# Where sixteen joins and eight statistics stand among the products of a mixture-of-experts layer

## The reference

```python
x = layernorm(x + attention(x))              # an online-gradient attention, 32 steps in sequence
gu = einsum('th,ehf->etf', x, w_gate_up)     # 8 experts, 2 of them for each token
routed = combine(silu(g) * u @ w_down)       # weights of the top two
shared = silu_and_mul(x @ w_sh_gate_up) @ w_sh_down      # one expert for all tokens, width 1024
x = layernorm(x + routed + shared)           # the last thing computed
```

## Time and profile before

| what | us |
|---|---|
| median of three runs | 683.67 |
| lowest and highest of them | 683.64, 685.2 |
| the profiled execution, whole | 685.18 |
| its span | 683.4 |
| TensorE busy in the span | 661.5 (97%) |
| VectorE busy | 450.9 (66%) |
| ScalarE busy | 316.7 (46%) |
| GpSimd busy | 308.0 (45%) |

### The profile page before, as it was taken

How to read it: one execution, slowest core, us unless ns; L and a number is a source line. 1 busy time by engine, 2 the same in 40 slices (tenths; PEclk the granted TensorE clock), 3 DMA queues, 4 the chain that set the end, 5 groups by cost and what they waited for, 6 DMA issues and landing times.

```text
span 683.4 us, 16572 instructions
## 1 busy us (share of the span) xinstructions
PE 661.5 (97%) x6792; PEld 527.2 (77%) x6792; DVE 450.9 (66%) x784; ACT 316.7 (46%) x552; POOL 308.0 (45%) x314
## 2 busy tenths in 40 slices
PE   9999999999999999999999999999999999999895
PEld 7767777776777777787887888888887888788684
DVE  5875865776844465398957544644466788888864
ACT  5343434445454432531033556755676554544353
POOL 0747657767735431011005335443552245665634
PEclk9999999999999999999999999999999999999998
DMA  8212233231542541100064578677549743253323
GB/s 280 91 35 77 84 100 98 97 112 52 160 128 81 156 139 36 46 0 1 1 246 117 178 265 296 207 249 261 181 165 348 268 148 93 93 184 94 108 78 123
DMA packets 66575, 93.53 MB, mean 137 GB/s; under 512 B 17024, under 2 KB 32128, under 8 KB 66496
## 3 DMA queue, kind: packets, MB, share of 16 engines
q1 hardware_dynamic: 60816, 73.81, 32.5%
q0 software_dynamic: 5680, 18.62, 9.3%
HBM read 68.61 MB, written 23.79 MB: 135 GB/s over the span
## 4 chain that ended last, share of the span: by engine, by line
PE 66%; DVE 15%; issue 7%; POOL 7%; ACT 4%; DVEq 0%; POOLq 0%; ACTq 0%
PE bank L1365 8%; PE bank L1216 7%; PE zbank L1439 6%; PE wbank L1439 6%; PE bank L1476 6%; PE bank L1271 4%; PE zbank L1324 3%; PE zbank L1353 3%; PE wbank L1324 3%; PE wbank L1353 2%; PE zbank L1452 2%; PE bank L1324 2%; PE wbank L1250 2%; PE zbank L1234 2%; POOL za L2062 2%
## 5 line engine op out<-in xcount | busy, mean ns | idle before, releaser
L2094 POOL TENSOR_TENSOR xl<-RAW,xh 128x1024 fp32r<-128x1024 f32 x23 | 55.5, 2411 | 123.0 <-ACT xh L1896 122.9
L2111 POOL DMA_INDIRECT xg<-x1d,idxu x39 | 42.1, 1079 | 71.1 <-DVE idxu L1024 41.2
L1977 ACT ACTIVATE ah<-sg 128x512 fp32r<-128x512 f32 x36 | 22.7, 632 | 107.2 <-DVE sg L1627 107.2
L1617 DVE TENSOR_TENSOR GL<-RAW,GH 128x1024 fp32r<-128x1024 f32 x36 | 43.2, 1224 | 11.0 <-ACT GH L1891 9.6
L1216 PE MATMUL bank<-xh,GH 128*128 128x512 f32 x112 | 47.7, 426 | 0.8 <-DVE kS L1517 0.8
L2136 POOL DMA_INDIRECT xg<-yd,SI x32 | 32.6, 1018 | 34.6 <-DVE x L1751 29.0
L1216 PE MATMUL bank<-xl,GH 128*128 128x512 f32 x112 | 44.1, 394 | 0.1
L1365 PE MATMUL bank<-xh,ah 128*128 128x512 f32 x104 | 42.1, 405 | 2.0 <-DVE x L1703 1.8
L1216 PE MATMUL bank<-xh,GL 128*128 128x512 f32 x112 | 43.9, 392 | 0.0
L1629 DVE TENSOR_TENSOR al<-sg,ah 128x512 fp32r<-128x512 f32 x36 | 27.0, 749 | 25.1 <-ACT ah L1977 25.1
L1365 PE MATMUL bank<-xh,al 128*128 128x512 f32 x104 | 40.7, 391 | 0.0
(11 more groups left out here) (387 smaller groups left out, 2029.5 us busy)
## 6 DMA issues: line engine op xcount, KB each, us to landing
RAW<-in_wgu SPq DMA_DIRECT2D x13, 1024.0 KB, 6.8
yd<-RAW SPq DMA_DIRECT2D x39, 256.0 KB, 5.3
RAW<-in_wsgu SPq DMA_DIRECT2D x14, 512.0 KB, 5.7
RAW<-in_wd SPq DMA_DIRECT2D x13, 512.0 KB, 5.9
xr<-in_xT SPq DMA_DIRECT2D x16, 256.0 KB, 4.6
x<-in_xtok SPq DMA_DIRECT2D x16, 256.0 KB, 4.3
x1d<-x SPq DMA_DIRECT2D x16, 256.0 KB, 2.7
RAW<-in_wsd SPq DMA_DIRECT2D x8, 512.0 KB, 5.6
```

The source lines that it names most:

```text
L1617: e.tensor_tensor(GL[:, w % 2, k:k + 2, :], gate_raw(w, k), GH[:, w % 2, k:k + 2, :].bitcast(F32), ALU.subtract).then_inc(*mark("low", "g" ...
L2094: e.tensor_tensor(DL[:, w % 2, :, :], draw[:, raw_of(w), :, :], DH[:, w % 2, :, :].bitcast(F32), ALU.subtract).then_inc(*mark("low p", "d" ...
L2111: e.indirect_dma_start(place(s), None, x1d, bass.IndirectOffsetOnAxis(ap=idxu[:, LINES[s]:LINES[s] + 1], axis=0)).then_inc(*mark(f"dma xg{ ...
```

## The change

Only the list of steps changes; every instruction stays. In `side`, join 11 goes from behind product 1 of block 6 to behind product 3, and the joins after it move on: 12 behind product 4 of block 6, 13 and 14 behind products 3 and 4 of block 7. Join 15 leaves the blocks: it now stands behind the third of the last eight tiles' down products, between the statistics of tiles 13 and 14. Preloads 10 and 11, which need joins 14 and 15, move with them. Of the statistics, those of tile 1 leave block 2 for block 3, those of 2 go to block 4, 3 stays there, 4 and 5 stand in block 5, 6 in block 6, 7 in block 7. So block 2 has one tile's statistics where it had two, and block 5 has two where it had one; blocks 3, 4, 6 and 7 keep their number.

```diff
-    side = {(2, 1): "f0", (2, 5): "f1", (2, 3): "j3", (2, 4): "j4", (3, 1): "f2", (3, 3): "j5", (3, 4): "j6", (4, 1): "f3", (4, 5): "f4", (4, 3): "j7",
-            (4, 4): "j8", (5, 1): "f5", (5, 3): "j9", (5, 4): "j10", (6, 1): "j11", (6, 5): "f6", (6, 3): "j12", (6, 4): "j13",
-            (7, 1): "f7", (7, 5): "j14", (7, 3): "j15"}
+    side = {(2, 1): "f0", (2, 3): "j3", (2, 4): "j4", (3, 1): "f1", (3, 3): "j5", (3, 4): "j6", (4, 1): "f2", (4, 5): "f3", (4, 3): "j7",
+            (4, 4): "j8", (5, 1): "f4", (5, 5): "f5", (5, 3): "j9", (5, 4): "j10", (6, 1): "f6", (6, 3): "j11", (6, 4): "j12",
+            (7, 1): "f7", (7, 3): "j13", (7, 4): "j14"}
...
-    for n in range(4):
-        preload(8 + n, FREE[n])
+    preload(8, FREE[0])
+    preload(9, FREE[1])
...
     for n, i in enumerate(last_down(3, 3, (4, 5, 6, 7))):
+        if n == 0:
+            preload(10, FREE[2])
+        if n == 2:
+            join(15)
+            preload(11, FREE[3])
         finish(i, 4 + n)
```

## The result

| | before | changed |
|---|---|---|
| median, us (7 runs each) | 684.75 (683.64 to 685.97) | 681.99 (681.29 to 682.33) |
| ratio, 95% interval | | 0.9962 (0.9952 to 0.9972) |
| profiled execution, span | 683.4 | 680.3 |
| M: block 2's first matmul to the last tile's division | 107.73 | 104.77 |
| D: the last tile's statistics to its division | 1.90 | 3.41 |

The account below looks back on a forecast made before the run. TensorE, busy in 97% of the span, was taken as the bound, so only its waits and the end counted. -4.2 - 0.8 + 0.5 + 1.1 = -3.4 us took the median from 683.67 to 680.3 us, range 679.2 to 683.0.

Parts of the forecast that it names:

- Block 6, -4.2: Block 6: without join 11 ahead of add 5, TensorE's wait and the slow matmuls behind it go, -4.2 us.
- Block 2, -0.8: Block 2: one tile's statistics fewer, add 5 earlier, the wait for add 7 gone, no collision, -0.8 us.
- The tie that I had worked out: Block 2: GpSimd's power instruction at 577.77 against VectorE's `pairs` subtraction at 577.76; GpSimd should lose.
- The rival: Block 2: GpSimd's big subtraction first, holding VectorE's mix low; +1.1 in place of -0.8, 682.2 us; chance 0.14.
- Block 5, +0.5: Block 5: a second pair of statistics ahead of add 5 makes product 3 later, +0.5 us, 0.8 at most.
- The end, +1.1: Last tiles: late join 14 and join 15 delay the statistics and GpSimd's small instructions, +1.1 us, between 0.4 and 1.6.
- join 14's 0.4: End: join 14 starts tile 12's statistics 0.7 us late; GpSimd wins back 0.35, so at least 0.4 remains.
- join 15's 0.7: End: the share of the +1.1 us put on join 15, between the statistics of tiles 13 and 14.
- nobody is held: End: case in which join 15 and GpSimd's small instructions do not block each other; the cost stays at 0.4 us.
- held to the join's end: End: case in which GpSimd's small instructions wait for join 15; tile 14's start 1.2 to 1.7 us late, less 0.25.
- The clock in block 2: Block 2 rival: GpSimd wins, TensorE idles some 1.4 us and its clock falls; 683.9 us, chance 0.07.
- the three pairs agree: Evidence for block 2's ties: three earlier VectorE and GpSimd pairs fit the rule that the second issued is blocked.

Follow-up runs that it names:

- split in block 7: Kernel before, with only the last down weight's split moved from block 6, product 1, to block 7, product 2; 681.04 us, ratio 0.9950.
- statistics back: Changed kernel with the statistics of tiles 1 to 5 back where they were, joins as changed; 682.82 us in one run.
- block 2 empty: Changed kernel with no statistics in block 2, all of them one place later; 683.45 us in one run.

## Why the prediction was right, point by point

- *Block 6, -4.2:* 4.18. The wait and the lower clock behind it are both gone. The hold of the mix low came as written (until 0.56 us behind GpSimd's end, 638.69 to 639.25), and add 7 was in time by 0.99, forecast 0.9. That GpSimd's subtraction beside the join was the cause, which the rows of before only suggested, is shown by the split in block 7. That the slow matmuls were the lower clock is shown by the granted clock of the kernel before: 1.00 of full speed until 641.9, 0.50 from 642.05 to 645.2, and 1.00 again from 645.6 on.
- *Block 2, -0.8:* 0.87, and no collision. The size is right; that the ties fell this way was in part luck. The tie that I had worked out, at the power instruction, did not take place: a gather ahead of it took 1.22 us instead of the 0.94 of before, so that already the first small instruction was late and was held behind the `pairs` subtraction. And one pair, the one at 623.77, did not settle how a tie goes: in the same profile, at 227.41, a tie of two wide instructions went against VectorE (last section). That VectorE comes first in the ties with GpSimd's 128x1 instructions was only shown by the runs. The rival was real; with GpSimd's small instructions gone from block 2, its subtraction was first by 0.09 us and that cost 1.35.
- *Block 5, +0.5:* 0.48.
- *The end, +1.1:* 1.51, the one term that was mis-sized. Its parts: join 14's 0.4 measured 0.39, so join 15's 0.7 is what failed; it measured 1.12. I had taken a value between "nobody is held" and "held to the join's end", with no row that chose between them; the rows show the second, two small instructions held in turn, and 0.2 us of waiting for the gather besides. It lay within the bounds of 0.4 to 1.6.
- *The sum:* -3.4 forecast; M says -2.96. The terms give -4.18 - 0.87 + 0.48 + 1.51 = -3.06, and 0.1 is lost in block 7. The ratio says -2.6 us (-3.3 to -1.9). The 680.3 us stood on a median of three runs that was 1.1 us under that of seven, from which the same sum would have given 681.35. The measured 681.99 is inside the range of 679.2 to 683.0, but 0.4 us above the forecast's own range of 679.2 to 681.6. The 0.38% are beyond the 0.3% that "faster" asked for; the weaker end of the interval, 0.28%, is just short of it.
- *The clock in block 2* did not come into it, and in the forced collision 0.84 us of idle time left it up. The prediction had put some 1.4 us of idle time there; no run here has that much.

The Trainium skill, "SBUF — State Buffer", section "Who interferes with whom", has the later of the two blocked for the whole of the earlier. Where the earlier one is VectorE's, or GpSimd's large subtraction, the rows of the changed kernel and of the experiments agree: small instructions are held behind VectorE's (1.28, 0.74, 0.82, 0.72 us) and VectorE's behind GpSimd's (1.48, 2.85). Two things do not agree. Where GpSimd's 128x1 instruction was 0.13 to 0.36 us ahead, in both kernels, VectorE was not held: above, the power instruction at 578.96 and the mix low at 579.30 overlap and take 0.57 and 0.68 us, as they do alone. The second pair of the earlier trace rows is such a case, so the prediction's "the three pairs agree" holds for two of them. And the join of block 6 in the kernel before, which began 0.51 us earlier than GpSimd's subtraction, was held all the same. No run here explains that. A gather instruction ahead of it on GpSimd is not enough: in the split in block 7 the join starts at 635.58 beside a gather from 635.12 to 636.07, and takes 1.60 us.

## What to carry to other kernels

Look for a long VectorE row beside a GpSimd row before moving an instruction out of the way: here moving GpSimd's 2.4 us subtraction to another block gave 3.9 us by M, and moving the joins alone ("statistics back") 2.8, since the first left the end as it was. Small instructions on GpSimd can be what keeps it out of VectorE's way; taking them away can make the kernel slower (block 2 empty, 1.35 us). And where an engine's work per tile is within a few per cent of the pace, as 1.32 us against 1.36 here, most of a delay put in front of it is not won back; moving one instruction of 0.2 us to an engine with time was then worth the whole delay.

## What the runs showed that I had not expected

- An idle time of TensorE of 0.84 us (a gap of 1.2 between matmuls) left its clock at the higher level, 2.4 GHz, in "block 2 empty"; after 2.42 us it was at the lower, 1.2 GHz.
- How a tie goes can't be read from the starts of the rows. Where a 128x1 instruction of GpSimd and a VectorE instruction with two inputs in SBUF started within 0.03 us of each other, VectorE came first in all 21 pairs over twelve profiles, those left out in which GpSimd was already held by an earlier row (577.57 and 577.59 above, and the pair at 623.77 in the earlier trace rows, are two of them). Two wide ones start level at about 227 us in every profile: VectorE was held in ten, GpSimd in three. In the kernel before (VectorE held, 1.85 us instead of 0.69) and in "block 2 empty" (GpSimd held, 1.83 instead of 1.29), timelines:

```profile
227.41 1.85 DVE L1629 TENSOR_TENSOR al<-sg,ah 128x512 fp32r<-128x512 f32 x1 [0.70 <-ACT ah L1977]
227.41 1.29 POOL L2074 TENSOR_TENSOR x<-x,bias 128x512 f32<-128x512 f32 x1
```
```profile
227.10 0.69 DVE L1634 TENSOR_TENSOR al<-sg,ah 128x512 fp32r<-128x512 f32 x1 [0.69 <-ACT ah L1982]
227.11 1.83 POOL L2079 TENSOR_TENSOR x<-x,bias 128x512 f32<-128x512 f32 x1
```

- The part of the program that no kernel here changes moved block 2's first matmul between 568.46 and 570.04 us. A gain of 1 us in the end can't be read from one span.
